# A gated slot-attention and expert block: high parts read from the transposes, and the order of preparation, turns and last sums changed

## What is computed

```
slots = layernorm(x)
Pn = rmsnorm(ctx); k = Pn @ Wk.T; v = Pn @ Wv.T
3 times:
    q = rmsnorm(slots) @ Wq.T
    attn = softmax over the tokens' axis (-2) of (q k.T / 16)
    attn = attn / (row sum + 1e-6)
    slots = gru_cell(attn @ v, slots)          # gates r, z, n; weights wih, whh of 768 x 256
x = x + tanh(g0) * slots
h = layernorm(x)
scores = sigmoid(h @ gate_w.T)                 # 16 experts
each expert takes its 512 best tokens (top_k over the tokens):
    eo = (silu(xin @ gw.T + gb) * (xin @ up_w.T + up_b)) @ down_w.T + down_b   # inner size 1024
    out[ids] += eo * score
x = x + tanh(g1) * (out + shared silu-gated ffn of inner size 512)
```

## Time and profile before

| | |
|---|---|
| runs | 1127.68, 1128.96, 1129.37 us; median 1128.96 |
| profiled execution | 1127.19 us, its span 1125.5 us |
| TensorE busy | 1083.5 us, 96% (weight load 932.2, 83%) |
| VectorE busy | 784.5 us, 70% |
| ScalarE busy | 548.3 us, 49% |
| GpSimd busy | 341.6 us, 30% |
| DMA | 105.39 MB, mean 94 GB/s |

### The profile page before, as it was taken

One profiled execution on the slowest core, in us unless ns is written; L12 is line 12 of the kernel. 1 busy time (PEld: TensorE's weight loads), 2 busy tenths in 40 slices (PEclk: granted clock), 3 DMA queues, 4 the chain that ended last, 5 costly groups with the idle time before them and its releaser, 6 DMA issues.

```text
span 1125.5 us, 17695 instructions
## 1 busy us (share of the span) xinstructions
PE 1083.5 (96%) x6087; PEld 932.2 (83%) x6087; DVE 784.5 (70%) x1502; ACT 548.3 (49%) x829; POOL 341.6 (30%) x351
## 2 busy tenths in 40 slices
PE   6699999999999999999999999999999999999996
PEld 4477888888887877888888888888888888898896
DVE  7877677777779878888456665666656666656663
ACT  4364454535456843332454544545445455445442
POOL 6106244444405100000222333433423424234332
PEclk9899999999999999999999999999999999999998
DMA  7600101010316441221474445445345344344421
GB/s 243 137 14 1 38 10 29 10 29 11 99 52 189 140 155 19 29 38 20 95 248 130 106 125 146 102 125 147 88 139 150 89 135 117 114 145 112 117 34 20
DMA packets 61195, 105.39 MB, mean 94 GB/s; under 512 B 12000, under 2 KB 50144, under 8 KB 56800
## 3 DMA queue, kind: packets, MB, share of 16 engines
q1 hardware_dynamic: 43936, 83.05, 23.3%
q0 software_dynamic: 16512, 21.50, 11.8%
q10 hardware_dynamic: 704, 0.29, 0.1%
HBM read 74.11 MB, written 21.27 MB: 85 GB/s over the span
## 4 chain that ended last, share of the span: by engine, by line
PE 85%; DVE 10%; issue 2%; ACT 1%; DMA 1%; SPq 0%; POOL 0%; DVEq 0%; ACTq 0%
PE wide L1279 29%; PE down L1293 15%; PE wide L848 13%; PE wide L1132 8%; PE down L1144 4%; PE down L907 3%; PE wide L855 2%; PE wide L857 2%; PE wide L1325 2%; PE side L1265 1%; PE side L1116 1%; PE down L1339 1%; DVE pre L1690 1%; DVE dif L1701 1%; PE side L303 1%
## 5 line engine op out<-in xcount | busy, mean ns | idle before, releaser
L2231 DVE SCALAR_TENSOR_TENSOR hid<-wide,b_up,silu 128x512 f32<-128x512 f32 x120 | 90.2, 751 | 161.3 <-PE wide L1279 152.9
L1279 PE MATMUL wide<-xt_hi,w_hi 128*128 128x512 f32 x480 | 188.5, 393 | 0.0
L1279 PE MATMUL wide<-xt_lo,w_hi 128*128 128x512 f32 x480 | 187.8, 391 | 0.0
L1279 PE MATMUL wide<-xt_hi,w_lo 128*128 128x512 f32 x480 | 186.8, 389 | 0.0
L819 POOL DMA_INDIRECT out_tokens<-y,idx_out x64 | 111.4, 1741 | 222.9 <-DVE y L2212 175.6
L1646 ACT ACTIVATE silu<-wide,b_gate 128x512 f32<-128x512 f32 x120 | 82.3, 686 | 143.6 <-PE wide L1279 142.3
L1293 PE MATMUL down<-w_hi,hid_hi 128*128 128x256 f32 x480 | 136.5, 284 | 0.0
L1293 PE MATMUL down<-w_lo,hid_hi 128*128 128x256 f32 x480 | 135.7, 283 | 0.0
L1293 PE MATMUL down<-w_hi,hid_lo 128*128 128x256 f32 x480 | 135.7, 283 | 0.0
L1655 ACT ACTIVATE hid_hi<-hid 128x512 fp32r<-128x512 f32 x120 | 76.0, 633 | 100.4 <-DVE hid L2231 100.4
L2182 DVE TENSOR_TENSOR w_lo<-raw,w_hi 128x768 fp32r<-128x768 f32 x128 | 121.5, 949 | 2.5 <-ACT w_hi L1620 2.5
(11 more groups left out here) (319 smaller groups left out, 2277.4 us busy)
## 6 DMA issues: line engine op xcount, KB each, us to landing
raw<-in_w_expert SPq DMA_DIRECT2D x32, 1536.0 KB, 6.3
x_raw<-in_x SPq DMA_DIRECT2D x16, 256.0 KB, 7.1
out_tokens<-slots SPq DMA_DIRECT2D x16, 256.0 KB, 3.8
token_rows<-work SPq DMA_DIRECT2D x8, 512.0 KB, 3.0
out_tokens<-y POOLq DMA_DIRECT2D x8, 512.0 KB, 5.9
attn<-rms_c SPq DMA_DIRECT2D x24, 128.0 KB, 2.4
attn<-expo SPq DMA_DIRECT2D x24, 128.0 KB, 2.3
x_first<-in_x SPq DMA_DIRECT2D x8, 256.0 KB, 3.0
```

The costliest lines, as they stand in the source:

```text
L1279: last = nc.tensor.matmul(bank[:, f % 2, :], w[f // HALF_F][:, f % HALF_F, (c + k) * P:(c + k + 1) * P], x_[:, k, :], start=(m == 1), stop ...
L2231: nc.vector.scalar_tensor_tensor(hid[:, f % 2, :], eup[:, f % 2, :], b_up[:, bass.ds(e, 1), f:f + 1].rearrange("p a b -> p (a b)"), silu[: ...
```

## The change

1. Preparation. SyncE loads groups 0 to 3 of x first. The moves of the value weights are made per pair: 16 of 192 KB in place of 8 of 384 KB. GpSimd begins its low parts only when VectorE has made both of its normalisations. VectorE aggregates after each group's statistics, leaves the rms factors until the normalisations are issued, and makes low parts before copies; ScalarE's high parts read the transposes in PSUM directly, and for groups 1 and 3 it makes the copies to `slots` last. TensorE interleaves transposes, rms spreads, value weights and scores anew. The maximum is taken in two halves. The end of the second half's statistics, its aggregates and its roots stand behind the attention weights' low parts.
2. `turn_rec` is issued inside the next gru unit, behind the products of gate r, in all passes but the first.
3. `turn_h(7)` is issued ahead of the first hidden product.
4. The instruction that prepares a count is issued one step earlier, and `token_ids(0)` one step later.
5. The last expert: the last two steps are done block by block, the bias times the score is made ahead in steps 4 to 7, and one instruction makes the result of a block. Block 3 has a bank of its own.

```diff
@@ SyncE
-                load_raw(0)
-                load_raw(1)
+                for g in range(G1):
+                    load_raw(g)
+                weights(wv_sb, wv_t, l_wv)
                 weights(wq_sb, wq, l_wq)
-                load_raw(2)
-                load_raw(3)
-                weights(wv_sb, wv_t, l_wv)
...
-                sp.wait_ge(a_own, 1)
-                move_rows(vw_hi, vw_own[:, :, :].bitcast(F32))
-                sp.wait_ge(p_own, 1)
-                move_rows(vw_lo, vw_f)
+                for pair in range(PAIRS):
+                    sp.wait_ge(a_own, pair + 1)
+                    move_rows(vw_hi, vw_own[:, :, :].bitcast(F32), pair)
+                    sp.wait_ge(p_own, pair + 1)
+                    move_rows(vw_lo, vw_f, pair)
@@ GpSimd
+                pool.wait_ge(n_x, 2)
                 for b in range(B):
...
-                pool.wait_ge(n_x, 1)
@@ TensorE, gru_unit, half_iteration
                         from_attention(gate_r, c, False).then_inc(m_r, 1)
+                        if early is not None:
+                            early()
...
                     gru_unit(it, pair, 2, 0, (lambda: column_sums(s)) if softmax else None)
-                    if softmax:
-                        turn_rec(s)
...
-                    gru_unit(it, pair, 2, 1, spread_after_slots if softmax else None)
+                    gru_unit(it, pair, 2, 1, spread_after_slots if softmax else None,
+                             early=(lambda: turn_rec(s)) if softmax else None)
@@ TensorE, turn_first
                             pe.wait_ge(s_lo, n - 1)
+                            pe.wait_ge(s_s0, n - 1)
@@ TensorE, preparation
+                pe.wait_ge(l_wv, 16)
+                project(small_banks[2], wv_sb, pn_t)
                 pe.wait_ge(e_w, 1)
                 pe.wait_ge(l_wq, 16)
                 project(small_banks[0], wq_sb, kp_t)
-                pe.wait_ge(l_wv, 16)
-                project(small_banks[2], wv_sb, pn_t)
-                pe.wait_ge(l_wih, 16)
-                pe.wait_ge(e_w, 3)
-                for n in range(3):
-                    value_weights(n)
-                pe.wait_ge(e_w, 6)
-                turn_rms(0)
                 turn_first(0)
                 turn_first(2)
-                value_weights(3)
+                pe.wait_ge(l_wih, 16)
+                pe.wait_ge(e_w, 2)
+                value_weights(0)
+                value_weights(1)
+                pe.wait_ge(e_w, 3)
+                turn_rms(0)
+                turn_first(1)
                 spread_rms(0, 0)
-                turn_first(1)
+                turn_first(3)
                 spread_rms(0, 1)
-                turn_first(3)
+                value_weights(2)
                 pe.wait_ge(a_whi, B)
                 pe.wait_ge(p_wlo, B)
-                pe.wait_ge(e_w, 7)
-                scores(0, 0, (2, 4), True)
+                pe.wait_ge(e_w, 4)
+                scores(0, 0, (2, 4), True, (0,))
+                pe.wait_ge(a_rms, 2)
+                value_weights(3)
+                pe.wait_ge(e_w, 5)
+                scores(0, 0, (2, 4), True, (1,))
@@ TensorE, router, counts, last expert
-                into_hidden(0, 0, 0)
                 turn_h(7, (a_hlo, 6))
+                into_hidden(0, 0, 0)
...
-                    if i == EDGE + 6:
+                    if i == EDGE + 7:
                         token_ids(0)
...
-                for m in range(2 * FE - LAG, 2 * FE):
-                    out_of_last(E - 1, m)
+                for j in range(2):
+                    for m in range(2 * FE - LAG, 2 * FE):
+                        out_of_last(E - 1, m, (j,))
@@ ScalarE
                 def first_high(g):
                     sl = slice(g * GROUP, (g + 1) * GROUP)
-                    act.wait_ge(s_s0, FIRST.index(g) + 1)
-                    nc.scalar.activation(slots_hi[:, :, sl], slots[:, :, sl], ACT.Copy).then_inc(s_hi, 1)
+                    act.wait_ge(t_x, FIRST.index(g) + 1)
+                    nc.scalar.activation(slots_hi[:, :, sl], turn_banks(g), ACT.Copy).then_inc(s_hi, 1)
+
+                def slots_after_low(g):
+                    sl = slice(g * GROUP, (g + 1) * GROUP)
+                    act.wait_ge(s_lo, FIRST.index(g) + 1)
+                    nc.scalar.activation(slots[:, :, sl], turn_banks(g), ACT.Copy).then_inc(s_s0, 1)
...
+                def own_weights(pair):
+                    act.wait_ge(e_w, 5 + 2 * pair)
+                    nc.scalar.activation(vw_own[:, pair, :], vw_f[:, pair, :], ACT.Copy).then_inc(a_own, 1)
...
+                first_high(2)
                 normalise(3)
-                first_high(0)
-                first_high(2)
-                value_weights(3)
+                value_weights(0)
+                first_high(1)
+                value_weights(1)
+                first_high(3)
                 copy_rms(0, 0, True)
                 copy_rms(0, 1, True)
-                first_high(1)
-                first_high(3)
-                act.wait_ge(e_w, 7)
-                nc.scalar.activation(vw_own[:, :, :], vw_f[:, :, :], ACT.Copy).then_inc(a_own, 1)
+                slots_after_low(1)
+                slots_after_low(3)
+                own_weights(0)
+                value_weights(2)
+                value_weights(3)
+                own_weights(1)
...
-                gru_unit(0, 0, 1, 0, lambda: first_slots(6), (),
-                         (lambda: copy_rms(1, 0), lambda: first_slots(7)))
+                gru_unit(0, 0, 1, 0, lambda: first_slots(6), (lambda: copy_rms(1, 0), lambda: first_slots(7)))
@@ VectorE
-                first_stats(range(NT))
+                for g in range(G1):
+                    first_stats(range(g * BLK, (g + 1) * BLK))
+                    aggregate(range(g * BLK, (g + 1) * BLK))
...
-                first_slots(0)
-                first_slots(2)
-                first_low(0)
-                first_low(2)
-                first_slots(1)
-                first_slots(3)
                 first_low(1)
                 first_low(3)
                 scale_scores(0, 0, True)
-                first_stats(range(NT, NT + 7))
+                half_maximum(0)
+                first_stats(range(NT, NT + 3))
                 scale_scores(0, 1, True)
-                maximum(0)
-                first_stats(range(NT + 7, NT + 11))
+                half_maximum(1)
+                maximum_of_halves()
+                first_stats(range(NT + 3, NT + 6))
                 token_sum(0)
-                first_stats(range(NT + 11, NT + 16))
-                aggregate(stats1, mv1, var1)
+                first_stats(range(NT + 6, NT + 11))
                 csum_reciprocal(0)
...
                 attention_lo(0, 1)
+                first_stats(range(NT + 13, 2 * NT))
+                aggregate(range(NT, 2 * NT))
+                variances(mv1, var1)
                 reciprocal_roots(1, mv1, var1, rstd1, rtmp1, shift1)
@@ VectorE, counts and last expert
                     u = i * 2 + LAG
-                    bisect_count(u)
                     low_part(i + 1, f + 1)
                     bisect_keep(u)
                     bisect_count(u + 1)
                     hidden(i + LAG, f + LAG)
                     bisect_keep(u + 1)
+                    if more:
+                        bisect_count(u + LAG)
...
+                def last_bias(j):
+
+                    if j == 0:
+                        dve.wait_ge(p_sums, E)
+                        dve.wait_ge(v_wt, E)
+                        dve.wait_ge(l_bd, 16)
+                    nc.vector.tensor_scalar(y[:, j, :], b_down[:, E - 1, :], weight[:, j, :], None, ALU.mult)\
+                        .then_inc(k_out, 1)
+
+                def last_results(j, done):
+
+                    dve.wait_ge(k_dn, done)
+                    dve.wait_ge(k_out, BLK * (E - 1) + 2 + j)
+                    nc.vector.scalar_tensor_tensor(y[:, j, :], last_sums(j), weight[:, j, :], y[:, j, :], ALU.mult, ALU.add).then_inc(k_yo, 1)
...
+                    if FE - BLK <= m < FE:
+                        last_bias(m - (FE - BLK))
                     if m == FE + LAG:
-                        last_results(0)
-                last_results(1)
+                        last_results(0, (E + 1) * FE)
+                        last_results(1, (E + 1) * FE)
+                last_results(2, (E + 2) * FE)
+                last_results(3, (E + 2) * FE + LAG)
```

More of the change, by code:

```diff
@@ L473, in flamingo_kernel, with last_sums @@
             k_out, k_yo = sem("k_out"), sem("k_yo")
+            def last_sums(j):
+                return exps[:, 0, 0:D] if j == BLK - 1 else edown[:, j // 2, (j % 2) * D:(j % 2 + 1) * D]
             def group_of(g):
@@ L831, in _, with gru_unit @@
             def _(pe):
-                def gru_unit(it, pair, g4, c, between=None, parts=("slots", "attention")):
+                def gru_unit(it, pair, g4, c, between=None, parts=("slots", "attention"), early=None):
```

(34 more changed lines are left out.)

79 lines of the change are left out of this document (38 added, 41 removed).

## The result

The changed kernel takes 1117.08 us (median of 4; 1115.51, 1116.43, 1117.72, 1118.57), the kernel before 1129.16 beside it (median of 4). The ratio is 0.9895, 95% interval 0.9877 to 0.9912: 12.1 us faster, where 8.6 were forecast. A second set of five runs gave 1117.74 against 1129.03, ratio 0.9903 (0.9888 to 0.9919). One run of the kernel before, of those beside experiments 5 to 8, took 1908.91 us at a mean clock of 0.702; the ratios and intervals leave it out.

The account below looks back on a forecast made before the run. TensorE was taken as the bound, busy 96% of the span, so gains come from removed waits and time around its filled stretch. Terms 3.1 + 2.05 + 2.35 + 0.2 + 0.9 = 8.6 gave 1120.4 us, range 1117.0 to 1124.3.

Parts of the forecast that it names:

- More: Rival: clock stays high, TensorE finds the third count in time, slack behind the first unit holds: 11 to 12, 1117.5; chance 0.17.
- the slow rival: Value-weight transfers: each of 16 moves costs as much as one of eight, 13 us lost, about 1135; chance 0.04.
- the last one: Preparation: the change doesn't do what it says, high parts still wait, only GpSimd order helps: 1125.5 to 1127; chance 0.05.
- Part 1: Preparation: 2.8 us from weights landing earlier, less 0.85 given back, plus 1.1 at the rms row: 3.1 us gained.
- Transfers: Preparation's value-weight moves: 16 half-size moves start near 33.6, end at 51.2; congestion of 1.0 us goes.
- Given back: Deferred VectorE work behind the attention low parts: about 2.4 us late at the first gate, 0.85 at the second unit.
- Part 2: The reciprocal's turn inside the next unit, five of six passes: 2.05 us gained, bounds 0 and 3.
- the rival in which it waits everywhere: The reciprocal's spread waits in place of its turn in every pass, giving 0 or less: 1122.5; chance 0.10.
- Part 3: Last turn of h ahead of the first hidden product: the 2.4 us wait goes, 2.35 gained, bounds 1.5 and 2.4.
- Part 4: Counts and ids: 1.1 us wait at the third count goes, about 0.9 returns at the next; 0.2 gained.
- Part 5: Last expert: fewer products before the first result and one VectorE instruction instead of two, 0.9 us gained.
- the scatter lands late: Last expert: a scatter landing 4 us later holds VectorE and costs TensorE 3.65 us, 1124.1; chance 0.06.

Follow-up runs that it names:

- experiments 5 to 8: Four follow-up kernels: fillers in the kernel before, then merged moves, GpSimd's wait removed, and statistics moved earlier in filled changed kernels: 1128.43, 1119.57, 1115.73, 1114.32 us.
- experiment 7: Changed kernel with thirteen unread products in the preparation's gaps, GpSimd's new wait for both normalisations removed: 1115.73 us, against 1115.25 with the wait.
- experiment 6: Changed kernel with thirteen unread products in the preparation's gaps, 8 moves of 384 KB in place of 16 of 192 KB: 1119.57 us, against 1115.25.
- Experiment 9: Changed kernel with thirteen unread products in the preparation's gaps, `turn_rec` back between two units in passes 1 to 5: 1118.49 us, against 1115.25.
- experiment 10: Changed kernel with thirteen unread products in the preparation's gaps, first hidden product again ahead of `turn_h(7)`: 1120.36 us, against 1115.25.
- experiment 12: Changed kernel with thirteen unread products in the preparation's gaps, count preparation and `token_ids(0)` put back as before: 1116.21 us, against 1115.25.
- experiment 11: Changed kernel with thirteen unread products in the preparation's gaps, last expert as before: 1117.85 us, against 1115.25.
- filled variant: Kernel before, with nine unread products in TensorE's 2.4 us wait for the normalised x: 1128.43 us against 1128.74, ratio 1.0003.

## Why the prediction was right, and where it was not

**The result** lies in the range that was given, but at its lower edge: 1117.08 with 1117.0 as its end, and 12.1 us gained for 8.6. The rival called "More" (11 to 12) had the number; of its three conditions the first, a clock that stays high, held in some executions, and the other two didn't hold: a count is still waited for, and VectorE is late at the first unit. That the sum of 8.6 agrees so well with the two profiles is in part luck: the changed kernel's profile holds the long fall, and without it the same marks give 11.1 (1125.5 against 1114.4). One of the recorded chances is added wrongly: all but the slow rival's 0.04 and half of the last one's 0.05 is 0.935, not 0.92.

**Part 1, 3.1 forecast (bounds 1.0 and 5.0).** In the profiled execution 2.1 at the first attention product and 2.7 from 80 us on (the product at 81.59 stands at 78.86); in the execution without the fall 4.9 and 5.4, above the upper bound. Step by step:
- The normalisations end at 19.9; forecast 20.2. Right in size. The reason given for it, that GpSimd waits for the second normalisation, was wrong: experiment 7 took the wait away and nothing changed.
- Scores to end at 38.4 without a fall, 39.5 with: their last product ends at 38.05 and 40.56 (it starts at 37.66 and 40.17). **This is the step that failed**: "I count one such fall, which lengthens the work on the path by 1.1 (no fall: 0; ... 1.7)". The fall lasted from 28 to 34.9 and cost 2.5; and it is absent in some executions. A term that is 0 in one execution and 2.5 in the next was put in as a constant, and its bound was too low, since the stretch seen before (26.2 to 29.6) was taken for its length.
- Statistics: 0.75 forecast, 0.84 measured (the reciprocal at 46.38 for 47.22, with exponentials that began at 42.48 for 42.28, 0.2 later; from the exponentials on it is 1.04).
- Transfers: the moves done at 51.2 by the bytes; at the latest at 49.4. Forecast for it was the end of congestion, 1.0, and it came: 2.33 us from issue to landing, as later in the kernel. But the term is mis-sized for the executions without the fall: experiment 6, with the moves merged and the clock up, loses 4.3. The halves don't only end the congestion, they let the earlier scores through.
- Given back: `pre` was forecast 2.4 late, and 0.85 at the second unit. VectorE was late by 2.2 (60.44, and ScalarE's `hb` ready at 57.53 + 0.68), but TensorE, at its lower level behind the attention wait, lost only 0.65 on it (from 2.12 to 1.47 of lead). The 1.1 at the rms row came in full (from 1.47 to 2.58).

**Part 2, 2.05.** In the marks of the profiled execution 0.94 in pass 1 (forecast 0.85), 0.5 to 0.6 in each of passes 2 to 4 (0.52), 0.3 lost in pass 5 (forecast 0.35, for `add_x(0)`; 0.85 + 1.55 - 0.35 is the 2.05): 2.25. Experiment 9 gives 2.3 by its profile. The spread did wait in pass 1, 0.69 us, and nowhere else, as forecast; the rival in which it waits everywhere fell.

**Part 3, 2.35.** By the marks 2.5 (lead 4.98 at the spread of pass 5, 7.50 at the router). By experiment 10 it is 4.0, in an execution with the fall behind the wait: the wait was priced at its length, and the slower work behind it was left out. This is the second mis-sized term, of the same kind as the first.

**Part 4, 0.2.** By the marks 0.35 at the fourth count, of which 0.15 is left at the last hidden values; 0.3 by experiment 12's profile, in which some 0.1 is older. The wait went from the third count (1.07) to the fourth (0.84), as forecast.

**Part 5, 0.9.** 0.9 by the marks (lead 7.65 at the last hidden values, 8.54 at the scatter), 0.9 by experiment 11. In detail not quite: the last low part is waited for, 0.41 us, since one block's products no longer cover it; the shorter results made up for it.

The new wait of `last_bias(0)` did come, as the forecast had it. VectorE's timeline in the changed kernel:

```profile
1085.99 0.35 DVE L2315 TENSOR_SCALAR y<-b_down,weight 128x256 f32<-128x256 f32 x1 [2.80 <-POOLq L828]
```

VectorE stood for 2.80 us until GpSimd's scatter had landed, and the next low part ended at 1087.64, 0.4 before TensorE's next result products (1088.07), for 0.35 forecast. TensorE lost nothing, and the rival "the scatter lands late" did not come; but the slack is no larger than it was reckoned.

**The rule against the change.** The first rival, 16 moves at the price of eight (2.05 each), needed a landing after 59.6 to lose; the last was down by 49.4. The Trainium skill ("SBUF — State Buffer", Summary: rules for kernel authors) advises one DMA rather than several for a transfer that bounds. Experiment 6 went the other way by 4.3 us: the transfer does bound there, but its parts are ready at different times, and the first half left 2.9 us sooner. Halves that leave as late as the merged moves were not run.

**Why 12.1 and not 8.6.** The profile of before is one of its shorter executions (1127.19, 2.0 under the median of 1129.16), that of the changed kernel its longest (1118.57, 1.5 over the median of 1117.08): that makes the 3.5. A removed wait takes away the fall of the clock behind it besides its own time, in the executions that have one: shown for the turn of h, by undoing it. In the preparation, filling the gaps of the changed kernel shows what its own fall costs, not that the change removed one. That the kernel before has such falls at 422 us in its own longer runs was seen only in its filled variant; no profile of the kernel before itself shows it, so this share is argued, not shown.

## What to carry to other kernels

A wait of TensorE of two microseconds is worth more than its length when the clock falls behind it (here 2.4 us of wait and 1.6 of slower work): price it with the work right behind it at half speed too, and look at several executions before taking a profile's clock for the program's. When one engine's deferred work moves behind a wait that is long anyway, look whether a slower clock is what hides it; if that goes, the lateness appears. Where a transfer bounds and its parts are ready at different times, try pieces that leave as they are ready. And where a profile agrees with a forecast to the tenth, look whether it is a typical execution.

## What was not expected of the hardware

The same program had the lower level from 28 to 34.9 us in one execution and not in another, with waits of the same length right ahead of it (1.69 and 1.60 us): 2.5 us of difference. The two had parted before that: from 12.3 us on eight equal records took 0.38 us each in one and 0.63 in the other, and the idle time behind them was 2.54 us and 0.79. Which of these brings the fall is open. Thirteen products of 0.23 us that nobody reads, put into the later waits, brought four executions to within 0.6 us of each other, and four of experiment 7, with the same fillers, to within 2.0.
